# A gate of eight between the attention gathers of a graph network: two semaphores a buffer

## The chip, the cores and the metric

One core of one Trainium2 chip runs the whole program in one launch. The core has five engines with queues of their own: PE (matrix products), DVE (vector work), ACT (activations and copies), POOL (here it computes the descriptors of the indirect transfers) and SP (it only issues transfers). They share 16 DMA engines and signal one another through semaphores. The metric is device time in microseconds, as the median of several executions.

## What is computed

Eight layers over 3,125 nodes of 256 features and 103,125 edges. The change concerns only the first, an attention over the edges with 8 heads of 32 numbers:

```python
q = (nfeat @ Wq.T).reshape(n, HEADS, HEAD_DIM) / SCALING
k = (nfeat @ Wk.T).reshape(n, HEADS, HEAD_DIM)
v = (nfeat @ Wv.T).reshape(n, HEADS, HEAD_DIM)
attn = jnp.einsum('ehd,ehd->eh', k[src], q[dst])
attn = attn + attn_bias
m = jax.ops.segment_max(attn, dst, num_segments=n)
a = jnp.exp(attn - m[dst])
s = jax.ops.segment_sum(a, dst, num_segments=n)
a = a / s[dst]
out = jax.ops.segment_sum(v[src] * a[:, :, None], dst, num_segments=n)
return out.reshape(n, FEAT) @ Wo.T
```

`k[src]` and `v[src]` are read edge by edge, 2 KB for each edge (256 keys and 256 values in fp32), and they are most of what this layer moves. After it come a mixture of experts, a second graph layer and so on, up to the output.

## The kernel before, in words

A first phase sorts the nodes by their number of incoming edges and writes a table `kv` to HBM, one row of 512 numbers (key, value) for each node. `attention_phase` then works through it. Its nodes stand in 25 tiles of 128, one node on each partition. The edges of a tile are cut into **bodies** of R = 8 edges a node; a plan that is computed on the chip says how many bodies each tile has, and in the executions here there are 116.

A body `b` uses one of SETS = 4 gather buffers, `got[k]` with k = b % 4, and one of two sets v = b % 2 of everything else. A loop runs over groups of four bodies (29 here), the same on all engines:

- POOL waits for the body's indices (`index_ready`) and for its buffer (`released[k]`), and then issues eight indirect gathers (L1942), each of which brings one edge's row for each of 128 nodes: 128 x 2 KB = 256 KB. All eight raise the semaphore `gathered[k]`, by 16 each. Its waits go through `wait_apart` (L1930), which follows each wait with an increment of a semaphore of its own, so that the wait is not merged into the transfer's instruction.
- DVE waits for `gathered[k]` (L2045), multiplies keys and queries (L2046), sums over a head (L2049), takes the running maximum (L2052, L2054), and multiplies the values by the weights that ACT has exponentiated (L2057). This last operation raises `released[k]`: the buffer is free. Then it waits for ACT's `keep_ready` and for PE's `summed` of the body before, scales that sum (L2063) and raises `messages_ready` (L2065).
- PE adds the body's eight messages and the scaled earlier sum in PSUM with nine products against the identity (L1998), and raises `summed` with the last of them. The records show 18 instructions for the nine.
- ACT exponentiates (L1973 to L1978), prepares the next body's queries and biases (L1957, L1959), computes the indices for the body four later (L1952, `index_ready`), and copies the finished sum out of PSUM (L1962).
- SP stores that sum to HBM (L1914).

Ahead of the change four buffers are thus the only bound on POOL: it may run up to four bodies ahead of DVE, whatever has landed of them.

Of the kernel before, what the change touches and what calls it, by code (L numbers as in the profile page):

```python
# [63 lines left out]
def rows_at(ap):  # L64
    return bass.IndirectOffsetOnAxis(ap=ap, axis=0)
# [1346 lines left out]
R = 8  # L1412
SETS = 4
SLOTS = 64
MAIN = SLOTS // R


ALL_TILES = TILES + 3
# [18 lines left out]

ALL_BODIES = TILES * MAIN + 2 * SETS + SETS

# [36 lines left out]
def front_phase(nc, name, a, ends_dram, keys_dram, order_dram, perm, counts, natural, place, main_bodies, edges, kv_dram,  # L1476
                q_dram):

    with ExitStack() as ctx:
# [81 lines left out]
        with nc.Block() as block:  # L1561
# [147 lines left out]
            def _(dve):  # L1709
# [117 lines left out]
                table = counts[:].rearrange("p (k c) -> p k c", c=2)  # L1827
                dve.tensor_scalar(main_bodies[:], bodies[:, 0:TILES], float(MAIN), None, ALU.min)
                dve.tensor_scalar(table[:, :, N_EXTRA], bodies[0:1, :], float(MAIN), 0.0, ALU.subtract, ALU.max)
                dve.drain()  # L1830
# [14 lines left out]
def attention_phase(nc, name, a, perm, main_bodies, edges, kv_dram, q_dram, state_dram):  # L1845
# [3 lines left out]
    with ExitStack() as ctx:  # L1849
        s = Scope(nc, ctx, name)  # L1850
# [3 lines left out]
        index = [s.sb(f"index{k}", [P, R], i32) for k in range(SETS)]  # L1854
# [25 lines left out]
        plan_ready = s.sem("plan_ready")  # L1880
        q_loaded = s.sem("q_loaded")
        index_ready = s.sem("index_ready")
        gathered = [s.sem(f"gathered{k}") for k in range(SETS)]
        released = [s.sem(f"released{k}") for k in range(SETS)]
        pool_waited = s.sem("pool_waited")
        staged = s.sem("staged")
# [11 lines left out]
        def group_count(eng):  # L1898
            return eng.value_load(groups[0:1, 0:1], min_val=1, max_val=TILES * MAIN // SETS)

        with nc.Block() as block:

            @block.sync
            def _(sp):
                sp.dma_start(ident[:], a["ident"]).then_inc(const_loaded, 16)
                sp.wait_ge(plan_ready, 1)
                with sp.Fori(0, group_count(sp)) as g:
                    for k in range(SETS):
                        b = g * SETS + k
                        t = sp.value_load(tile_of[0:1, bass.ds(b, 1)], min_val=0, max_val=TILES)  # L1910
                        sp.wait_ge(out_ready, b + 3)

                        sp.wait_ge(stored, 16 * b + 32)
                        sp.dma_start(state_dram[bass.ds(t * P, P), :], out[k % 2][:]).then_inc(stored, 16)  # L1914
                sp.wait_ge(stored, group_count(sp) * (16 * SETS) + 32)
                sp.sem_inc(all_stored, 1)

            @block.gpsimd
            def _(pool):
                pool.iota(number[:], [[1, ALL_BODIES]], base=0, channel_multiplier=0, allow_small_or_imprecise_dtypes=True)  # L1920
                pool.drain().then_inc(number_set, 1)
                for k in range(SETS):
                    pool.sem_inc(released[k], 1)
                pool.sem_inc(out_ready, 1)
                pool.sem_inc(stored, 32)
                for k in range(TILES):
                    pool.indirect_dma_start(out=q[:, k, :], out_offset=None, in_=q_dram,
                                            in_offset=rows_at(perm[:, k, NODE:NODE + 1])).then_inc(q_loaded, 16)

                def wait_apart(sem, value):  # L1930


                    pool.wait_ge(sem, value)
                    pool.sem_inc(pool_waited, 1)

                wait_apart(plan_ready, 1)
                with pool.Fori(0, group_count(pool)) as g:
                    for k in range(SETS):
                        wait_apart(index_ready, g * SETS + (k + 1))
                        wait_apart(released[k], g + 1)  # L1940
                        for r in range(R):
                            pool.indirect_dma_start(out=got[k][:, r, :], out_offset=None, in_=kv_dram,  # L1942
                                                    in_offset=rows_at(index[k][:, r:r + 1])).then_inc(gathered[k], 16)

            @block.scalar
            def _(act):
                def piece(b):
                    return act.value_load(piece_of[0:1, bass.ds(b, 1)], min_val=0, max_val=TILES * MAIN - 1)

# [4 lines left out]
                def stage(b, v):  # L1954

                    at = piece(b)
                    act.activation(p_q[v][:, 0:F].rearrange("p (a n) -> p a n", a=1), q[:, bass.ds(at // MAIN, 1), :],  # L1957
                                   ACT.Copy, scale=SCALE)
# [45 lines left out]
            def _(dve):  # L2004
                def over(ap, shape, pattern, **kw):
                    return ap.rearrange(pattern, **kw).to_broadcast(shape)
# [31 lines left out]
                with dve.Fori(0, group_count(dve)) as g:  # L2038
                    for k in range(SETS):
                        b, v = g * SETS + k, k % 2  # L2040
                        keys = got[k][:, :, 0:F].rearrange("p r (h d) -> p r h d", h=HEADS)
                        values = got[k][:, :, F:2 * F].rearrange("p r (h d) -> p r h d", h=HEADS)
                        wide = [P, R, HEADS, HD]
                        dve.wait_ge(gathered[k], g * (16 * R) + 16 * R)
                        dve.wait_ge(staged, b + 1)  # L2045
                        dve.tensor_tensor(prod[v][:, :, :, 0:HD], keys,  # L2046
                                          over(p_q[v][:, 0:F], wide, "p (a h d) -> p a h d", a=1, h=HEADS), ALU.mult)
                        dve.drain()
                        dve.tensor_reduce(score[v][:, 0:R, :].rearrange("p r h -> p (r h)"),  # L2049
                                          prod[v][:].rearrange("p r h d -> p (r h) d"), AX.X, ALU.add)  # L2050
                        dve.drain()
                        dve.tensor_reduce(peak[v][:], score[v][:].rearrange("p r h -> p h r"), AX.X, ALU.max)  # L2052
                        dve.drain()
                        dve.tensor_tensor(score[v][:], score[v][:], over(peak[v][:], [P, R + 1, HEADS], "p (a h) -> p a h", a=1),  # L2054
                                          ALU.subtract).then_inc(shifted, 1)
                        dve.wait_ge(weights_ready, b + 1)
                        dve.tensor_tensor(msg[v][:, 0:R, :, 0:HD], values,  # L2057
                                          over(p_weight[v][:, 0:R * HEADS], wide, "p (r h a) -> p r h a", h=HEADS, a=1),
                                          ALU.mult).then_inc(released[k], 1)

                        dve.wait_ge(keep_ready, b + 1)
                        dve.wait_ge(summed, b + 1)
                        dve.tensor_tensor(msg[v][:, R, :, :], p_msg[1 - v][:, 0:MSG].rearrange("p (h d) -> p h d", h=HEADS),  # L2063
                                          over(keep[v][:], [P, HEADS, HD + 1], "p (h a) -> p h a", a=1), ALU.mult)
                        dve.drain().then_inc(messages_ready, 1)  # L2065
# [894 lines left out]
```

## Time and profile before

| | |
|---|---|
| Median of 3 runs | 4707.68 us |
| Lowest and highest of them | 4687.77 and 4724.29 us |
| The profiled execution | 4710.12 us, its span 4708.6 us |
| PE busy in the span | 3059.3 us (65%) |
| DVE busy | 2428.8 us (52%) |
| POOL busy | 1425.6 us (30%) |
| ACT busy | 1172.6 us (25%) |
| Moved by the DMA engines | 616.26 MB, mean 131 GB/s |

The times of instructions come from one profiled execution. A timeline counts microseconds from the start of the span. A row gives the start, the duration, the engine, the source line, the operation with its output and inputs (buffer numbers left out, so that `gnn_got` is any of the four buffers), and in brackets how long the engine had been idle before it and what the profile takes to have ended that. "issue" there means that the profile shows nothing that was waited for. A releaser is inferred from the semaphore's number, and numbers are used again by later phases: a name out of the first phase inside the attention loop is such a number's earlier use. Waits, register steps and branches are done by an engine's sequencer and have no rows of their own here.

### The profile page before, as it was taken

What the parts mean: (1) busy time and instruction counts of PE and PEld (TensorE: products, weight loads), DVE (VectorE), ACT (ScalarE), POOL (GpSimd) and SP (SyncE); (2) the same over time, 40 slices, a digit from 0 to 9 for tenths busy, and PEclk for the clock granted to TensorE, in tenths of its full rate; (3) what the DMA queues carried; (4) which work ended last, traced back from release to release, by engine and by line L of the source; (5) the groups of instructions that cost most, each with busy time, mean ns of one, the idle gap of its engine ahead of it and who ended that gap; (6) DMA issues with size and microseconds to landing.
All of it is one profiled execution on the core that took longest, in us unless ns stands there. A gap on an engine that the chain in (4) does not pass through costs nothing. (4 is left out here: it accounts for less than half of the span.)

```text
span 4708.6 us, 51834 instructions
## 1 busy us (share of the span) xinstructions
PE 3059.3 (65%) x15437; PEld 2517.8 (53%) x15437; DVE 2428.8 (52%) x4181; ACT 1172.6 (25%) x2483; POOL 1425.6 (30%) x1393
## 2 busy tenths in 40 slices
PE   4234444444444445485688873999975996499598
PEld 2123333333333334364688863777764886388587
DVE  7345555555555564443799974111133665323343
ACT  1111111111111111121255541333322553000122
POOL 4655555555555542544430000000000000001133
PEclk8667777777777777697899995999987998699799
DMA  2555555556655655243353344000017443455333
GB/s 87 160 166 171 171 171 170 168 161 174 174 168 168 174 146 197 86 71 84 109 201 167 167 168 144 17 11 11 6 51 138 140 135 108 166 205 181 124 64 53
DMA packets 293112, 616.26 MB, mean 131 GB/s; under 512 B 52284, under 2 KB 198976, under 8 KB 283040
## 3 DMA queue, kind: packets, MB, share of 16 engines
q0 software_dynamic: 105584, 294.01, 23.0%
q1 hardware_dynamic: 170080, 270.39, 16.8%
q10 hardware_dynamic: 17360, 50.80, 3.6%
q8 instruction: 42, 0.69, 0.1%
q14 instruction: 46, 0.38, 0.0%
HBM read 440.73 MB, written 176.95 MB: 131 GB/s over the span
## 5 line engine op out<-in xcount | busy, mean ns | idle before, releaser
L1998 PE MATMUL gnn_p_msg<-gnn_msg,gnn_ident 128*128 128x264 f32 x2088 | 675.0, 493 | 947.1 <-issue 710.1
L1998 PEld LDWEIGHTS gnn_p_msg<-gnn_msg,gnn_ident 128*128 128x128 f32 x2088 | 510.5, 250 | 1111.5 <-issue 737.9
L1942 POOL DMA_INDIRECT gnn_got<-kv,gnn_index x928 | 877.7, 946 | 648.0 <-DVE gnn_msg L2057 376.4
L2438 PE MATMUL tables_p_pair<-tables_spread,tables_hot 128*128 128x100 f32 x3328 | 398.0, 279 | 18.4 <-DVE tables_spread L2412 16.8
L2438 PEld LDWEIGHTS tables_p_pair<-tables_spread,tables_hot 128*128 128x128 f32 x3328 | 383.5, 194 | 32.5 <-DVE tables_spread L2412 29.9
L2063 DVE TENSOR_TENSOR gnn_msg<-gnn_p_msg,gnn_keep 128x264 f32<-128x264 f32 x116 | 49.6, 428 | 534.0 <-DMA front_w<-in_L_gnn_Wq 397.9
L2719 PE MATMUL gnn_p_sum<-gnn_hs,gnn_edge 128*128 x2500 | 288.9, 278 | 34.5 <-DVE gnn_edge L2749 34.0
L2719 PEld LDWEIGHTS gnn_p_sum<-gnn_hs,gnn_edge 128*128 128x128 f32 x2500 | 285.3, 194 | 39.3 <-issue 38.9
L2046 DVE TENSOR_TENSOR gnn_prod<-gnn_got,gnn_p_q 128x2048 f32<-128x2048 f32 x116 | 265.4, 2288 | 66.6 <-issue 34.8
L1087 PE MATMUL ffn_pA<-ffn_hw,ffn_slabs 128*128 128x256 f32 x1250 | 275.2, 382 | 32.6 <-DMA ffn_beta<-in_L_ffn_beta 32.6
L683 DVE SCALAR_TENSOR_TENSOR ffn_acc<-ffn_pC,ffn_gates,ffn_acc 128x256 f32<-128x256 f32 x200 | 88.9, 480 | 395.8 <-PE ffn_pC L567 395.8
L487 ACT ACTIVATE ffn_h<-ffn_pA,ffn_hb,ffn_hs 128x384 f32<-128x384 f32 (+1 forms) x320 | 197.4, 617 | 352.9 <-PE ffn_pA L537 352.9
L2057 DVE TENSOR_TENSOR gnn_msg<-gnn_got,gnn_p_weight 128x2048 f32<-128x2048 f32 x116 | 265.5, 2289 | 34.1 <-issue 19.4
L2049 DVE TENSOR_REDUCE gnn_score<-gnn_prod 128x64 f32<-128x2112 f32 x116 | 272.9, 2353 | 8.6
L1087 PEld LDWEIGHTS ffn_pA<-ffn_hw,ffn_slabs 128*128 128x128 f32 x1250 | 238.3, 191 | 65.3 <-DMA ffn_beta<-in_L_ffn_beta 33.0
L2749 DVE SCALAR_TENSOR_TENSOR gnn_edge<-gnn_steep,gnn_cell 128x1152 f32<-128x1152 f32 (+1 forms) x150 | 190.5, 1270 | 132.6 <-PE gnn_p_sum L2719 80.3
L2410 DVE TENSOR_TENSOR tables_hot<-tables_low_c,tables_iota 128x1024 f32<-128x1024 f32 x208 | 253.5, 1219 | 0.0
L2695 ACT ACTIVATE gnn_steep<-gnn_number,gnn_minus 128x1152 f32<-128x1152 f32 (+1 forms) x150 | 177.4, 1184 | 151.8 <-DVEq L2751 115.5
L976 POOL DMA_INDIRECT by_expert<-ffn_xn,ffn_place_i x100 | 97.7, 977 | 374.3 <-DVEq L1258 346.1
L1962 ACT ACTIVATE gnn_out<-gnn_p_msg 128x264 f32<-128x264 f32 x117 | 45.7, 390 | 599.1 <-issue 530.0
L567 PE MATMUL ffn_pC<-ffn_wc,ffn_h 128*128 128x256 f32 x800 | 190.7, 396 | 4.4 <-DVE ffn_acc L672 4.4
L148 POOL MEMSET h_epsb<- 128x1 f32 x1 | 0.1, 98 | 624.3 <-POOLq L51 624.3
(413 smaller groups left out, 4802.8 us busy)
## 6 DMA issues: line engine op xcount, KB each, us to landing
weight_table<-tables_weight_slab SPq DMA_DIRECT2D x13, 3200.0 KB
count_table<-tables_count_row SPq DMA_DIRECT2D x13, 3200.0 KB
ffn_slabs<-weight_table SPq DMA_DIRECT2D x25, 1600.0 KB
gnn_cell<-count_table ACTq DMA_DIRECT2D x50, 576.0 KB, 3.8
state<-gnn_out SPq DMA_DIRECT2D x116, 136.0 KB
ffn_xs<-by_expert SPq DMA_DIRECT2D x60, 260.0 KB, 3.3
gnn_got<-kv,gnn_index POOLq DMA_INDIRECT x928
ffn_x<-x SPq DMA_DIRECT2D x20, 640.0 KB
```

The source lines that it names most:

```text
L487: act.activation(to[:, m, t0 * P:t1 * P], pA[:, j % 4, 0:(t1 - t0) * P], hidden_act[layer][0], bias=hb[layer][:, e, m:m + 1], scale=scale) ...
L567: last = nc.tensor.matmul(pC[:, t * F:(t + 1) * F], last_h[:, k, t * P:(t + 1) * P], wc[:, e, k, :], start=(k == 0), stop=(k == KC - 1))
L1087: last = nc.tensor.matmul(pA[j % 2][:, 0:F], slabs[:, j % SLABS, b * P:(b + 1) * P], hw[:, b, :], start=(b == 0), stop=(b == TILES - 1))
L1942: pool.indirect_dma_start(out=got[k][:, r, :], out_offset=None, in_=kv_dram, in_offset=rows_at(index[k][:, r:r + 1])).then_inc(gathered[k] ...
L1998: last = nc.tensor.matmul(p_msg[v][:, 0:MSG], ident[:], msg[v][:, r].rearrange("p h d -> p (h d)"), start=(r == 0), stop=(r == R))
L2046: dve.tensor_tensor(prod[v][:, :, :, 0:HD], keys, over(p_q[v][:, 0:F], wide, "p (a h d) -> p a h d", a=1, h=HEADS), ALU.mult)
L2049: dve.tensor_reduce(score[v][:, 0:R, :].rearrange("p r h -> p (r h)"), prod[v][:].rearrange("p r h d -> p (r h) d"), AX.X, ALU.add)
L2057: dve.tensor_tensor(msg[v][:, 0:R, :, 0:HD], values, over(p_weight[v][:, 0:R * HEADS], wide, "p (r h a) -> p r h a", h=HEADS, a=1), ALU.mu ...
L2410: dve.tensor_tensor(hot[c % AHEAD][:], across_tiles(low_c[:, at], CHUNK, P), counting(CHUNK, P), ALU.is_equal)
L2438: last = nc.tensor.matmul(at, hot[c % AHEAD][:, r, :], spread[c % AHEAD][:, r, :], start=True, stop=True)
L2719: last = nc.tensor.matmul(p_sum[:, to:to + C], of[:, b * P:(b + 1) * P], rhs.rearrange("p a d -> p (a d)"), start=False, stop=False)
L2749: dve.scalar_tensor_tensor(edge[v][:, 0:w], steep[v][:, 0:w], 1.0, cell[k][:, 0:w], ALU.min, ALU.mult).then_inc(edge_ready, 1)
```

## The change

The gathers of a buffer raise two semaphores in place of one, the first four (half 0) and the last four (half 1). Ahead of each half of the buffers k = 1, 2 and 3 POOL now also waits until the same half of the buffer k - 1, of the same group, has landed. Buffer 0 has no such wait. DVE waits for both halves ahead of its first product, where it waited for one count.

```diff
+HALF_R = R // 2
...
-        gathered = [s.sem(f"gathered{k}") for k in range(SETS)]
+        gathered = [[s.sem(f"gathered{k}{h}") for h in range(2)] for k in range(SETS)]
...
                         wait_apart(index_ready, g * SETS + (k + 1))
                         wait_apart(released[k], g + 1)
                         for r in range(R):
+                            if k > 0 and r % HALF_R == 0:
+                                wait_apart(gathered[k - 1][r // HALF_R], g * (16 * HALF_R) + 16 * HALF_R)
                             pool.indirect_dma_start(out=got[k][:, r, :], out_offset=None, in_=kv_dram,
-                                                    in_offset=rows_at(index[k][:, r:r + 1])).then_inc(gathered[k], 16)
+                                                    in_offset=rows_at(index[k][:, r:r + 1])).then_inc(gathered[k][r // HALF_R], 16)
...
-                        dve.wait_ge(gathered[k], g * (16 * R) + 16 * R)
+                        for h in range(2):
+                            dve.wait_ge(gathered[k][h], g * (16 * HALF_R) + 16 * HALF_R)
                         dve.wait_ge(staged, b + 1)
```

On POOL, the buffers 0, 1 and 2 in the loop's body stand as follows. The semaphores in brackets go by the names under which the first phase used their numbers: `front_keys_loaded0` is `index_ready`, and the other one is `released[k]`. Before:

```order
L1942 DMA gnn0_got<-kv,gnn0_index0 128x512 [waits front_start_ready]
L1942 DMA gnn0_got<-kv,gnn0_index0 128x512 x7
L1933 REGISTER_ALU
L1942 DMA gnn0_got<-kv,gnn0_index1 128x512 [waits front_keys_loaded0,front_next_ready]
L1942 DMA gnn0_got<-kv,gnn0_index1 128x512 x7
L1933 REGISTER_ALU
L1942 DMA gnn0_got<-kv,gnn0_index2 128x512 [waits front_keys_loaded0,front_mine_ready]
L1942 DMA gnn0_got<-kv,gnn0_index2 128x512 x7
```

And with the change, where `front_keys_loaded1` and `front_keys_loaded2` are the two halves of buffer 0, `front_keys_loaded3` and `front_keys_loaded4` those of buffer 1:

```order
L1945 DMA gnn0_got<-kv,gnn0_index0 128x512 [waits front_place_ready]
L1945 DMA gnn0_got<-kv,gnn0_index0 128x512 x7
L1934 REGISTER_ALU
L1934 ISA [waits front_keys_loaded0,front_scattered]
L1945 DMA gnn0_got<-kv,gnn0_index1 128x512 [waits front_keys_loaded1]
L1945 DMA gnn0_got<-kv,gnn0_index1 128x512 x3
L1945 DMA gnn0_got<-kv,gnn0_index1 128x512 [waits front_keys_loaded2]
L1945 DMA gnn0_got<-kv,gnn0_index1 128x512 x3
L1934 REGISTER_ALU
L1945 DMA gnn0_got<-kv,gnn0_index2 128x512 [waits front_keys_loaded0,front_perm_loaded,front_keys_loaded3]
L1945 DMA gnn0_got<-kv,gnn0_index2 128x512 x3
L1945 DMA gnn0_got<-kv,gnn0_index2 128x512 [waits front_keys_loaded4]
```

The eight gathers of buffers 1 and 2 are now two runs of four with a wait ahead of each; those of buffer 0 are as they were.

On DVE, the start of a body (k = 1) stands so before, `front_keys_loaded2` being `gathered[1]` and `front_scattered` being `staged`:

```order
L2045 REGISTER_ALU [waits front_keys_loaded2]
L2046 TENSOR_TENSOR gnn0_prod1<-gnn0_got,gnn0_p_q1 128x64x32 [waits front_scattered]
```

And with the change, where `front_done` is `staged`:

```order
L2049 REGISTER_ALU [waits front_keys_loaded4,front_keys_loaded3]
L2050 TENSOR_TENSOR gnn0_prod1<-gnn0_got,gnn0_p_q1 128x64x32 [waits front_done]
```

The register step has two waits in place of one; the operations behind it are unchanged, and nothing moves between engines.

## Rows read from the trace of the kernel before

**Rows 1.** Table of stretches: busy us (count) by engine, clock, DMA share, GB/s
```profile
core 0: us, PE busy (x) PEld busy (x) DVE busy (x) ACT busy (x) POOL busy (x), PEclk, DMA share, GB/s
240.00:1765.00 1525.00, 665.15 (x2053) 503.08 (x2054) 895.17 (x690) 268.33 (x1063) 865.02 (x915) 0.72 0.58 168
```

**Rows 2.** Groups by line, 235 to 1773 us: count, busy us, mean ns, idle before
```profile
L1942 POOL DMA_INDIRECT gnn_got<-kv,gnn_index x919 | 869.2, 946 | 645.3 <-DVE gnn_msg L2057 376.4 <-issue 267.6 <-ACT gnn_index L1952 1.2
L2049 DVE TENSOR_REDUCE gnn_score<-gnn_prod 128x64 f32<-128x2112 f32 x116 | 272.9, 2353 | 8.6
L2057 DVE TENSOR_TENSOR gnn_msg<-gnn_got,gnn_p_weight 128x2048 f32<-128x2048 f32 x116 | 265.5, 2289 | 34.1 <-issue 19.4 <-ACT gnn_p_weight L1973 14.7
L2046 DVE TENSOR_TENSOR gnn_prod<-gnn_got,gnn_p_q 128x2048 f32<-128x2048 f32 x116 | 265.4, 2288 | 66.6 <-issue 34.8 <-DMA gnn_got<-kv,gnn_index 31.8
L2063 DVE TENSOR_TENSOR gnn_msg<-gnn_p_msg,gnn_keep 128x264 f32<-128x264 f32 x116 | 49.6, 428 | 534.0 <-DMA front_w<-in_L_gnn_Wq 397.9 <-issue 136.1
```

**Rows 3.** Waits, 235 to 1773 us: total us, times, longest us
```profile
DVE gnn_msg L2063 <- DMA front_w<-in_L_gnn_Wq: 397.9, 28, 27.8
POOL gnn_got L1942 <- DVE gnn_msg L2057: 376.4, 44, 20.9
DVE gnn_msg L2063 <- issue: 136.1, 10, 15.1
DVE gnn_prod L2046 <- DMA gnn_got<-kv,gnn_index: 31.8, 2, 30.0
```

**Rows 4.** Timeline of one cycle: start us, us, engine, line, operation, idle before
```profile
1025.40 0.43 DVE L2063 TENSOR_TENSOR gnn_msg<-gnn_p_msg,gnn_keep 128x264 f32<-128x264 f32 x1 [16.42 <-DMA front_w<-in_L_gnn_Wq]
1033.92 0.42 DVE L2063 TENSOR_TENSOR gnn_msg<-gnn_p_msg,gnn_keep 128x264 f32<-128x264 f32 x1
...
1034.79 0.94 POOL L1942 DMA_INDIRECT gnn_got<-kv,gnn_index  x1 [12.61 <-DVE gnn_msg L2057]
...
1042.44 0.42 DVE L2063 TENSOR_TENSOR gnn_msg<-gnn_p_msg,gnn_keep 128x264 f32<-128x264 f32 x1
1042.95 6.64 PE L1998 MATMUL gnn_p_msg<-gnn_msg,gnn_ident 128*128 128x264 f32 x18 [4.24 <-issue]
1043.08 2.29 DVE L2046 TENSOR_TENSOR gnn_prod<-gnn_got,gnn_p_q 128x2048 f32<-128x2048 f32 x1 [0.21 <-issue]
1048.75 2.29 DVE L2057 TENSOR_TENSOR gnn_msg<-gnn_got,gnn_p_weight 128x2048 f32<-128x2048 f32 x1 [0.29 <-issue]
1048.94 0.30 ACT L1978 ACTIVATE gnn_msg<-gnn_score 128x64 f32<-128x64 f32 x1
1062.33 0.43 DVE L2063 TENSOR_TENSOR gnn_msg<-gnn_p_msg,gnn_keep 128x264 f32<-128x264 f32 x1 [11.29 <-DMA front_w<-in_L_gnn_Wq]
1063.34 2.29 DVE L2046 TENSOR_TENSOR gnn_prod<-gnn_got,gnn_p_q 128x2048 f32<-128x2048 f32 x1 [0.58 <-issue]
1063.60 0.95 POOL L1942 DMA_INDIRECT gnn_got<-kv,gnn_index  x1 [0.30 <-issue]
1072.10 0.94 POOL L1942 DMA_INDIRECT gnn_got<-kv,gnn_index  x1 [7.55 <-DVE gnn_msg L2057]
```

**Rows 5.** Timeline of the burst before that one: two buffers' boundaries and the end
```profile
1002.38 0.95 POOL L1942 DMA_INDIRECT gnn_got<-kv,gnn_index  x1 [0.30 <-issue]
1011.34 0.21 ACT L1952 ACTIVATE gnn_index<-edges 128x8 int32 x1 [3.25 <-issue]
1012.49 0.94 POOL L1942 DMA_INDIRECT gnn_got<-kv,gnn_index  x1 [0.42 <-issue]
1021.24 0.94 POOL L1942 DMA_INDIRECT gnn_got<-kv,gnn_index  x1 [0.30 <-issue]
```

**Rows 6.** Timeline of the loop's start: the eighth gather, and DVE's first product
```profile
232.15 0.95 POOL L1942 DMA_INDIRECT gnn_got<-kv,gnn_index  x1 [0.30 <-issue]
235.94 2.29 DVE L2046 TENSOR_TENSOR gnn_prod<-gnn_got,gnn_p_q 128x2048 f32<-128x2048 f32 x1 [30.04 <-DMA gnn_got<-kv,gnn_index]
```

**Rows 7.** The line L2046: ns min/median/max, first and last start us
```profile
L2046 DVE TENSOR_TENSOR gnn_prod<-gnn_got,gnn_p_q x116: 2286/2289/2290, 235.9 to 1764.8; 128x2048 f32<-128x2048 f32 x116
```

**Rows 8.** Table of stretches, columns as in rows 1: inside a burst and at its end
```profile
1001.00:1006.00 5.00, 5.00 (x18) 3.80 (x17) 4.85 (x3) 1.17 (x1) 3.78 (x4) 0.76 0.81 234
1006.00:1011.00 5.00, 0.19 (x1) 0.00 (x0) 2.61 (x3) 1.41 (x7) 3.78 (x4) 0.92 0.72 211
1016.00:1021.00 5.00, 0.00 (x0) 0.00 (x0) 0.00 (x0) 0.00 (x0) 3.78 (x4) 0.50 0.77 212
1023.00:1024.00 1.00, 0.00 (x0) 0.00 (x0) 0.00 (x0) 0.00 (x0) 0.00 (x0) 0.50 0.78 234
1024.00:1025.00 1.00, 0.00 (x0) 0.00 (x0) 0.00 (x0) 0.00 (x0) 0.00 (x0) 0.50 0.13 49
1025.00:1026.00 1.00, 0.09 (x1) 0.09 (x1) 0.43 (x1) 0.11 (x1) 0.00 (x0) 0.50 0.00 0
```

## Prediction

> **What bounds the kernel now.** I read the table of stretches first. The attention loop, from 240 to 1765 us, is 1,525 of the 4,708.6 us, and in it no engine is full: DVE is busy for 895 us, POOL for 865 us, PE for 665 us, and the DMA engines for 0.58 of the time [rows 1]. Outside it nothing is edited. Then the groups by line, for what one body costs (a body is 8 gathers of 128 rows into one of four buffers, and the arithmetic on them). The 919 gathers counted there take 946 ns each; DVE's three large operations take 2.3 us each; and DVE stands idle for 534.0 us ahead of L2063, in a loop of 116 bodies [rows 2]. The waits say who was waited for: POOL stood for 376.4 us until DVE's L2057 released a buffer, and DVE stood for only 31.8 us, twice, for a gather; its idle time at L2063 is 28 + 10 = 38 stalls of 14 us [rows 3]. So gathered data is almost never late, and POOL's idle time is DVE's stall handed back through the four buffers.
>
> One cycle shows how. DVE runs three bodies 8.52 us apart (L2063 at 1025.40, 1033.92, 1042.44), ends L2057 at 1051.04 and then stands until 1062.33 [rows 4]. L2063 waits in the code for ACT's `keep_ready`, last raised by the operation that ended at 1049.24, and for PE's `summed`, raised by a product whose 18 records end at 1049.59. Both had ended by then. The label "DMA front_w" on that row is an old user of a semaphore number and no transfer that L2063 waits for. That PE's is the late one, by 12.7 us, is my reading: ACT's signals pass in a stall (its index of 1011.55 starts a gather at 1012.49, while DVE stands [rows 5]). POOL meanwhile issues 24 gathers without a break, every 1.25 us from 1034.79 to 1063.60, then has no free buffer until DVE ends another L2057, and starts again at 1072.10. The cycle is thus 9.4 us from DVE's restart at 1025.40 to POOL's at 1034.79, and then the burst of 24 x 1.25 = 30 us, less what DVE restarts before its end (2.5 us here): 37 us in this one, and over the loop 1,529 us (L2046 from 235.94 to 1764.8 [rows 6, 7]) in 38 stalls, 40 us. Why PE's signal is late no row says. It is late only in the second half of a burst, and it comes near the burst's end.
>
> **The change part by part.** The gate is the first part. Six half-buffers of a group (k = 1, 2, 3, two halves each) get a wait, 6 x 29 groups = 174. The gate of a half asks for the same half of the buffer before. The last gather of that half started five gathers earlier, 5 x 1.25 = 6.25 us. When has a gather landed? Two places bound it. In the first body the eighth gather starts at 232.15 and DVE, which waits for just that, starts at 235.94 [rows 6]: 3.8 us. At the end of a burst the last gather starts at 1021.24, the DMA engines are at 0.78 until 1024, 0.13 until 1025 and 0.00 after it [rows 5, 8]: at most 3.8 us again. So the neighbour's half is down 6.25 - 3.8 = 2.45 us before the gated gather would start anyway. How early must it be? The gather at 1012.49 is one that waited, for the index that ACT's operation at 1011.34 gives after 0.21 us: 0.94 us from signal to start, with an idle of 0.42 us in place of 0.30. The boundary of two buffers eight gathers before it, at 1002.38, had the same two waits already met and stands at 0.30 like every other gather [rows 5]. So a met wait costs POOL nothing, because it lies under the gather that runs, and the gate has 2.45 - 0.94 = 1.5 us to spare. After a break of POOL the neighbour is older still. With 3.8 us from start to landing and one start each 1.25 us, about three gathers are in flight at any time; a bound of eight does not bind. I take 0 for the gates. The bounds: 174 x 0.12 us = 21 us if each costs what the late index cost, and no gain, if nothing in the burst moves.
>
> The Trainium skill's page "DMA: Bandwidth & Descriptors", section "Anatomy of one DMA — SWDGE (gpsimd) path", speaks against any gate of this kind: a transfer's fixed cost is mostly the receipt of its last write, which the semaphore has to wait for, about 2.0 us beside the bytes at 436 GB/s. A gate puts that receipt on the issuing engine's path. For these 256 KB an estimate from the page is 2.6 us, less than the 3.8 us that the rows show, and by either the gate opens in time.
>
> DVE's wait is the second part: one wait ahead of L2046 becomes two (one each half), 116 times, each met long before in the loop. There the idle time is 0.21 us in most bodies and 0.58 us after a jump back, and it holds a drain's end, a register step and the wait [rows 4]. The trace has no row for one wait alone. From below it costs nothing; from above the whole 0.21 us again, 116 x 0.21 = 24 us. I take a third, 0.07 us, because the gap is made of three things: 8 us. Only one body in three has DVE ahead of POOL's restart, so a third of that, 3 us, is what the cycle sees if the stall absorbs the rest. Between 3 and 8 us I take 6. PE, ACT and SP keep their orders; four more semaphores are cleared in the same place.
>
> The sum against the profiled execution: 1.5 us around the span, 4708.6 + 1.5 + 0 + 6 = 4716. That execution is 2.4 us over the median of the three runs (4707.68), so against the median it is 4714. The runs lie from 4687.77 to 4724.29, and a difference under 1% is what cannot be told from none here.
>
> **The rivals.**
> The gate calms the burst (faster). The stall belongs to bursts: PE's signal was quick at 1034 and 1042 and late after twelve gathers in a row, while the DMA engines stood at 0.72 to 0.81 [rows 8]. If the gates broke the stream often enough, the signal would not be late. Without any stall POOL sets the pace, 116 x 8 x 1.25 = 1,160 us in place of 1,529: 369 us less, 4347. With half of the stalls gone it is 4530. Against it: a gate that opens 1.5 us early breaks nothing. 13 in 100, most of it for a part of the gain.
> The gate binds (slower). It decides from the point where a gather needs more than 6.25 - 0.94 = 5.3 us from its start to a landing that POOL can see. In the burst nobody waits for a gather, so the 3.8 us come from its two ends alone. If it were 6.3 us in its middle, every gate would cost 1 us: 174 us, 4890; at 5.8 us it is 87 us, 4803. For it speaks only that one signal, PE's, is late just there; against it that the bytes keep moving at over 200 GB/s to the end and nothing is left a microsecond after 1024 [rows 8]. 11 in 100.
> The rhythm locks otherwise. The stalls come once in three bodies (38 in 116 bodies). If a small shift of the waits made it one in four, 9 fewer would be 126 us less (4590); one in two, 20 more would be 280 us more (4996). Nothing in the rows asks for either. 3 in 100 each way.
> The added waits cost their upper bounds: 21 + 24 = 45 us, 4755. This is inside the forecast's own range and just within 1%.
>
> **How the numbers follow.** The forecast, 4714, that the gates are met and nothing moves, has 70 in 100; its own range is 4680 to 4758, from the spread of the runs and the upper bounds of the waits. The calmed burst has 13, the binding gate 11, the other rhythm 6. Faster by over 1% is the first rival and half of the last but one: 0.16. Slower is the second and the other half: 0.14. Within 1%: 0.70. For 8 in 10 the range reaches down to a third of the stalls gone, 4714 - 369 / 3 = 4591, said as 4600, and up to gates at a little under half a microsecond each, 4714 + 76 = 4790.
>
> **What the profile of the changed kernel would show.** If I am right: gathers 1.25 us apart across half-buffer boundaries, with an idle of 0.30 us; bursts of 24; DVE's idle ahead of L2063 (now L2067) still near 534 us in some 38 stalls; POOL waiting for L2057 (now L2061) for some 376 us; no idle time of POOL put down to a DMA. Ahead of the first product of a body DVE would show near 0.28 us in place of 0.21. I am wrong at the gates if POOL shows waits on its own gathers, and wrong about the burst if the stalls grow fewer or shorter while its gathers keep their spacing. Wrong altogether would be a loop of 116 bodies that ends before 1650 us or after 1850 us.

## The result and the profile after

The changed kernel takes 4720.66 us in the median (20 runs, 4691.24 to 4738.19), the kernel before 4706.90 us in 20 runs of the same sessions: a ratio of 1.0031, 95% interval 1.0019 to 1.0042. So it is about 14 us slower, 9 to 20 us, and within 1%. The forecast was 4714.

The profiled execution has a span of 4715.9 us. Its page shows the same busy times as before, and its attention loop, from the first to the last start of DVE's first product, is 1,541.0 us where it was 1,528.9 [rows 7]. That is 12 us more; the rest of the span is 5 us less. The line, as the profile tells it by source line (ns min/median/max, first and last start us):

```profile
L2050 DVE TENSOR_TENSOR gnn_prod<-gnn_got,gnn_p_q x116: 2286/2289/2291, 234.7 to 1775.7; 128x2048 f32<-128x2048 f32 x116
```

The groups by line, 235 to 1785 us, with columns as in rows 2; the edit moved every line by three or four:

```profile
L1945 POOL DMA_INDIRECT gnn_got<-kv,gnn_index x918 | 868.0, 946 | 652.6 <-DVE gnn_msg L2061 370.3 <-issue 275.3 <-ACT gnn_index L1955 4.0
L2053 DVE TENSOR_REDUCE gnn_score<-gnn_prod 128x64 f32<-128x2112 f32 x116 | 272.9, 2353 | 8.5
L2061 DVE TENSOR_TENSOR gnn_msg<-gnn_got,gnn_p_weight 128x2048 f32<-128x2048 f32 x116 | 265.5, 2289 | 34.1 <-issue 19.1 <-ACT gnn_p_weight L1976 15.0
L2050 DVE TENSOR_TENSOR gnn_prod<-gnn_got,gnn_p_q 128x2048 f32<-128x2048 f32 x116 | 265.5, 2289 | 74.4 <-issue 42.6 <-DMA gnn_got<-kv,gnn_index 31.9
L2067 DVE TENSOR_TENSOR gnn_msg<-gnn_p_msg,gnn_keep 128x264 f32<-128x264 f32 x116 | 49.6, 428 | 537.8 <-DMA front_rows_in<-in_x 386.8 <-issue 151.0
```

Against [rows 2] two numbers on DVE have moved: the idle time ahead of the first product by 7.8 us (66.6 to 74.4), and that ahead of the operation with the stalls by 3.8 us (534.0 to 537.8). POOL waits for DVE's release for 370.3 us, where it was 376.4. The waits of the same stretch (total us, times, longest):

```profile
DVE gnn_msg L2067 <- DMA front_rows_in<-in_x: 386.8, 28, 27.0
POOL gnn_got L1945 <- DVE gnn_msg L2061: 370.3, 38, 21.0
DVE gnn_msg L2067 <- issue: 151.0, 12, 14.6
POOL gnn_got L1945 <- DMA gnn_got<-kv,gnn_index: 3.0, 10, 0.3
```

The last row looks like gates that bind, but its longest is 0.3 us, the ordinary idle time between two gathers: a landing happened to fall into it. A piece of one cycle (timeline):

```profile
1017.79 0.94 POOL L1945 DMA_INDIRECT gnn_got<-kv,gnn_index  x1 [0.30 <-issue]
1018.39 2.29 DVE L2061 TENSOR_TENSOR gnn_msg<-gnn_got,gnn_p_weight 128x2048 f32<-128x2048 f32 x1 [0.29 <-issue]
1019.04 0.95 POOL L1945 DMA_INDIRECT gnn_got<-kv,gnn_index  x1 [0.30 <-issue]
...
1032.79 0.95 POOL L1945 DMA_INDIRECT gnn_got<-kv,gnn_index  x1 [0.30 <-issue]
1035.04 0.43 DVE L2067 TENSOR_TENSOR gnn_msg<-gnn_p_msg,gnn_keep 128x264 f32<-128x264 f32 x1 [14.36 <-DMA front_rows_in<-in_x]
1035.75 2.29 DVE L2050 TENSOR_TENSOR gnn_prod<-gnn_got,gnn_p_q 128x2048 f32<-128x2048 f32 x1 [0.28 <-issue]
1044.59 0.94 POOL L1945 DMA_INDIRECT gnn_got<-kv,gnn_index  x1 [10.86 <-DVE gnn_msg L2061]
```

It is the picture of [rows 4]: gathers every 1.25 us across all half-buffer boundaries (the median idle time ahead of a gather is 0.305 us at each of the eight places in a buffer, before and after), DVE stalled from the end of L2061 (1020.68) to 1035.04, POOL without a buffer until 1044.59. The gap ahead of DVE's product is 0.28 us, where it was 0.21.

### The profile page after: what moved, and what is told of

Read it like the earlier page. It is cut to its first block and busy times, and to the rows that moved or that the text cites. A ratio compares the mean times of both kernels' runs of the same rounds, so it can differ in the third digit from the quotient of the medians.

```text
span 4715.9 us, 52153 instructions
## 1 busy us (share of the span) xinstructions
PE 3051.7 (65%) x15437; PEld 2515.0 (53%) x15437; DVE 2429.5 (52%) x4181; ACT 1172.7 (25%) x2483; POOL 1425.3 (30%) x1393
## 2 busy tenths in 40 slices
DMA packets 293112, 616.26 MB, mean 131 GB/s; under 512 B 52284, under 2 KB 198976, under 8 KB 283040
## 5 line engine op out<-in xcount | busy, mean ns | idle before, releaser
L1945 POOL DMA_INDIRECT gnn_got<-kv,gnn_index x928 | 877.4, 946 | 655.6 <-DVE gnn_msg L2061 370.3
L2067 DVE TENSOR_TENSOR gnn_msg<-gnn_p_msg,gnn_keep 128x264 f32<-128x264 f32 x116 | 49.6, 428 | 537.8 <-DMA front_rows_in<-in_x 386.8
L2050 DVE TENSOR_TENSOR gnn_prod<-gnn_got,gnn_p_q 128x2048 f32<-128x2048 f32 x116 | 265.5, 2289 | 74.4 <-issue 42.6
L2061 DVE TENSOR_TENSOR gnn_msg<-gnn_got,gnn_p_weight 128x2048 f32<-128x2048 f32 x116 | 265.5, 2289 | 34.1 <-issue 19.1
```

The lines of the kernel that those rows point to most:

```text
L2050: dve.tensor_tensor(prod[v][:, :, :, 0:HD], keys, over(p_q[v][:, 0:F], wide, "p (a h d) -> p a h d", a=1, h=HEADS), ALU.mult)
L2061: dve.tensor_tensor(msg[v][:, 0:R, :, 0:HD], values, over(p_weight[v][:, 0:R * HEADS], wide, "p (r h a) -> p r h a", h=HEADS, a=1), ALU.mu ...
```

## The experiments

Three sessions, each with runs of the kernel before on its own chip; ratios are against those. Only the session of the result has a trace of the kernel before, so an idle time that is set beside [rows 2] is compared across sessions; in the first of the three the kernel before takes 4730.07 us in the median, 23 us more than above. A diff is cut to the line that makes the experiment; what goes with it elsewhere (more semaphores and DVE's waits on them, another operand, the zeroing) is left out. Two questions: what the 14 us are made of, and whether a gate could do more than this one.

### The two parts, each alone

DVE's second wait without the gates, an edit of the changed kernel:

```diff
-                            if k > 0 and r % HALF_R == 0:
-                                wait_apart(gathered[k - 1][r // HALF_R], g * (16 * HALF_R) + 16 * HALF_R)
```

> The change without its gates: two semaphores a buffer, and DVE waits for both, POOL waits for none of its own gathers. Theory (the cost of the change is DVE's second wait, the gates are met and free): DVE's idle time ahead of its first product stays at the 74 us of the changed kernel, against 67 us before, and the time is that of the changed kernel, 10 to 16 us over before. Rival (the gates cost it): the time is that of before, within 5 us.

Measured: 4737.66 against 4730.07 us, a ratio of 1.0015, interval 0.9997 to 1.0032: 8 us more, between -1 and 15. The idle time ahead of DVE's product is 74.3 us, as in the changed kernel, so the second wait is 0.07 us in each body. That part of the theory holds. The time decides nothing: 8 us lies between the theory's 10 to 16 and the rival's 5, and the interval takes in both, and none at all.

POOL's waits without DVE's, to the kernel before:

```diff
+                            if k > 0 and r % (R // 2) == 0:
+                                wait_apart(released[k], g + 1)
```

> The kernel before with six more waits a group on POOL at the places of the gates, each for a semaphore that the same engine has already waited for (the buffer's release), so that each is met. Theory: a met wait lies under the gather that runs; gathers stay 1.25 us apart and the time is that of before, within 5 us. Rival (the gates cost POOL time by being there): up to 174 x 0.12 = 21 us more, with idle times of 0.42 us at half-buffer boundaries.

Measured: 4741.64 us, a ratio of 1.0023, interval 1.0009 to 1.0037: 11.6 us more, 4 to 17. Neither side of the expectation holds as it was put: the median idle time ahead of a gather is still 0.305 us at each half-buffer boundary, as the theory has it, and yet the kernel is slower, by more than the theory's 5 us in the median (5 us is inside the interval). To see whether this is real, the same wait stands ahead of seven of each body's eight gathers (`if r > 0:`), 812 in all:

> The kernel before with seven more waits a body on POOL, each long met: 812 in place of the change's 174. Theory (a met wait lies under the gather that runs, and what the six a group cost was noise): within 8 us of before. Rival (each instruction or signal on POOL inside a burst adds to what holds the others back, 11.6 us for 174): 4.7 times as much, 40 to 60 us over before.

Measured: 4747.29 against 4710.72 us, a ratio of 1.0084, interval 1.0061 to 1.0107: 37 us more by the medians, 40 by the ratio, 29 to 50 by the interval. The theory falls, and the rival holds at the low end of its 40 to 60 us. The groups by line of this kernel, 235 to 1810 us:

```profile
L1944 POOL DMA_INDIRECT gnn_got<-kv,gnn_index x919 | 869.2, 946 | 674.0 <-DVE gnn_msg L2059 378.6 <-issue 285.3 <-ACT gnn_index L1954 10.1
L2065 DVE TENSOR_TENSOR gnn_msg<-gnn_p_msg,gnn_keep 128x264 f32<-128x264 f32 x116 | 49.6, 428 | 562.8 <-DMA front_w<-in_L_gnn_Wq 456.6 <-issue 105.8 <-PE gnn_p_msg L2000 0.2
```

Inside a buffer POOL's gathers are no further apart (0.305 us of idle time in the median at each place). Ahead of a buffer's first gather they are, now and then: 21 of the 116 idle times there lie between 0.35 and 4 us, where 4 do in the trace before and 4 in the changed kernel, and POOL's "issue" time is 285.3 us where it was 267.6. By the timelines each of the 21 ends a microsecond or less after that buffer's index or its release, as for the late index of the prediction. One of them (timeline, ACT's index at L1954):

```profile
1028.27 0.21 ACT L1954 ACTIVATE gnn_index<-edges 128x8 int32 x1 [3.42 <-issue]
1029.42 0.94 POOL L1944 DMA_INDIRECT gnn_got<-kv,gnn_index  x1 [0.61 <-issue]
```

On DVE only the idle time at the stall grew, 562.8 us against 534.0 in [rows 2], and that is the whole of the 29 us by which the loop is longer (1,557.9 us against 1,528.9). So a met wait on POOL costs about 0.05 us (39 / 812), and it is paid on other engines: in DVE's stall, and in indices of ACT that come late. Two things stay open. Each of these waits stands with an increment of a semaphore (`wait_apart`), and no run parts the two. And the stall differs between sessions too: 559.0 us in the half-bytes kernel below, which has no wait added. For 174 gates 0.05 us each is 8 us; the run of the 174 alone says 11.6, and its interval, 4 to 17 us, holds both.

### What the stall is made of

Three kernels change one suspected load each. First the bytes: rows of 1 KB out of the query table in place of 2 KB.

```diff
-                            pool.indirect_dma_start(out=got[k][:, r, :], out_offset=None, in_=kv_dram,
+                            pool.indirect_dma_start(out=got[k][:, r, 0:F], out_offset=None, in_=q_dram,
```

> The kernel before, whose gathers bring 1 KB rows of the query table in place of 2 KB rows of keys and values, with as many gathers of as many rows; DVE reads the same half twice. Theory (what holds PE's signal back is the load of the bytes on the DMA engines): the stalls of 14 us ahead of L2063 are gone or much shorter, POOL is the bound at 10 us a body, and the loop takes 1,160 to 1,250 us in place of 1,529: 4,340 to 4,430. Rival (it is the number of packets, signals or records in a burst, not their bytes): the stalls stay, 4,700.

Measured: 4721.01 us, 0.9975 (0.9958 to 0.9993). The rival holds: half of the gathered bytes are worth 0.25%. The waits of this kernel, 235 to 1800 us:

```profile
DVE gnn_msg L2063 <- DMA front_w<-in_L_gnn_Wq: 507.6, 34, 28.5
POOL gnn_got L1942 <- DVE gnn_msg L2057: 397.5, 37, 20.8
DVE gnn_msg L2063 <- issue: 51.3, 4, 12.9
```

38 stalls, as before, and 559 us. Then PE's own instructions, two products in place of nine:

```diff
-                        for r in range(R + 1):
+                        for r in (0, R):
```

> The kernel before with two products a body on PE in place of nine (messages 1 to 7 are left out of the sum, and the weights in the denominator's column are ones). Theory A (the late signal waits behind something of PE's own instructions, 0.7 us for each of its 18, which gives 13 us): the stall shrinks with them to about 3 us, and the loop goes toward POOL's 1,160 us, 4,350 to 4,450 in all. Theory B (the signal is held until the burst of gathers ends, whatever PE did): each stall still ends near the burst's end, and the time stays within 1% of before.

Measured: 4512.66 us, 0.9537 (0.9512 to 0.9562). Theory B falls: the stalls ahead of L2063 are gone (1.1 us of idle time in all). Theory A has that right, but not the total of 4,350 to 4,450: the loop is 1,346 us and not 1,160, because the hold has gone to another engine. A timeline inside a burst:

```profile
1011.78 2.13 PE L1998 MATMUL gnn_p_msg<-gnn_msg,gnn_ident 128*128 128x264 f32 x4 [10.00 <-issue]
1017.91 0.39 ACT L1957 ACTIVATE gnn_p_q<-gnn_q 128x256 f32 x1 [6.77 <-issue]
1019.31 0.32 ACT L1959 ACTIVATE gnn_prod<-edges 128x64 f32 x1 [1.01 <-issue]
1019.66 2.29 DVE L2046 TENSOR_TENSOR gnn_prod<-gnn_got,gnn_p_q 128x2048 f32<-128x2048 f32 x1 [7.96 <-issue]
1024.71 0.94 POOL L1942 DMA_INDIRECT gnn_got<-kv,gnn_index  x1 [6.79 <-ACT gnn_index L1952]
```

Between its operations ACT has only a register to load in the code, and yet it is 6.77 us late; DVE waits for ACT, and POOL then waits for ACT's index (174.6 us in this kernel, 1.2 us before). That index is a second bound on POOL, beside the four buffers. So the stall is not a property of PE's products alone. My reading is that in a burst the instructions of several engines go through slowly, and that PE, which has the most of them in a body, shows it first; the rows show late ones on ACT and SP, and PE's late signal.

Last the number of gathers, four a body in place of eight:

```diff
-                        for r in range(R):
+                        for r in range(0, R, 2):
```

> The kernel before with four gathers a body in place of eight (every other edge's row is not fetched; the buffers are zeroed once, about 70 us ahead of the loop, and the arithmetic is unchanged). Half the bytes did not help while the packets stayed; here packets, bytes and POOL's time all halve. Theory (the number of transfers' packets in a stretch holds the other engines back): no stalls, DVE's 8.5 us a body is the bound, 116 x 8.5 = 990 us for the loop, 4,240 in all. Rival (something in the loop apart from the gathers causes the stall): stalls of 14 us once in three bodies stay, 4,750.

Measured: 4179.59 us, 0.8856 (0.8830 to 0.8881). The theory holds, though the total was put 60 us too high: the zeroing hides ahead of the loop, whose first product starts at 234.2 us (235.9 before). The loop is 996 us, DVE is the bound at 8.6 us a body, and the row that had 534.0 us of idle time has none (groups by line, 225 to 1250 us):

```profile
L2066 DVE TENSOR_TENSOR gnn_msg<-gnn_p_msg,gnn_keep 128x264 f32<-128x264 f32 x116 | 49.4, 426 | 0.0
```

So it is the number of gathers in a stretch that goes with the stalls, and not their bytes alone. Nor is it the DMA packets that the page counts: of 293,112 the half-bytes kernel has lost 30,816 and this one 37,120, nearly as many, and only this one has lost its stalls.

SP issues one store a body, and its issues tell of the stalls too, by their longest and not by their median. The row in the kernel before, in the one with 812 more waits, and with half of the gathers (ns min/median/max):

```profile
L1914 SPq DMA_DIRECT2D state<-gnn_out x116: 6/697/2087, 269.5 to 1778.1; - x116
```

```profile
L1914 SPq DMA_DIRECT2D state<-gnn_out x116: 8/336/1424, 270.5 to 1807.2; - x116
```

```profile
L1914 SPq DMA_DIRECT2D state<-gnn_out x116: 332/332/370, 258.2 to 1243.8; - x116
```

In the six kernels with stalls of 534 us and more the median is 692 to 700 ns three times and 336 to 339 three times, but the longest is 1,400 ns or more in each; in the four without them or nearly so (half of the gathers, spaced gathers, and two kernels with gates that bind, below) it is 370 to 719 ns.

### Gates that bind

The same gate at other distances. At one gather's distance, four in flight at most, each half waits for the one just before it:

```diff
-                            if k > 0 and r % HALF_R == 0:
-                                wait_apart(gathered[k - 1][r // HALF_R], g * (16 * HALF_R) + 16 * HALF_R)
+                            if r % HALF_R == 0 and (k, r) != (0, 0):
+                                j = 2 * k + r // HALF_R - 1
+                                wait_apart(gathered[j // 2][j % 2], g * (16 * HALF_R) + 16 * HALF_R)
```

> The gate at one gather's distance: each half waits for the half issued just before it, seven gates a group of four bodies, so that at most four gathers are in flight. My rule for a gate at a distance of d gathers is a cost of 3.8 + 0.94 - 1.25 d us if positive: 3.5 us here. Theory (nothing else moves): 203 gates x 3.5 us = 710 us more work for POOL, 1,870 us for the loop, about 340 us over before: 5,050 to 5,100. Rival (broken bursts free the other engines, the stalls of 14 us vanish and POOL's gates are all that is left): the same bound of POOL, 1,160 + 710 = 1,870, so the total tells little, but the stalls ahead of DVE's L2066 operation show it: none in place of 38. If the stalls stayed on top of the gates the loop would be over 2,200.

Measured: 5005.59 us, 1.0606 (1.0575 to 1.0637), a little under the forecast of my rule. Its timeline of POOL gives the gate's true price:

```profile
1001.70 0.95 POOL L1946 DMA_INDIRECT gnn_got<-kv,gnn_index  x1 [0.30 <-issue]
1002.95 0.95 POOL L1946 DMA_INDIRECT gnn_got<-kv,gnn_index  x1 [0.30 <-issue]
1007.37 0.94 POOL L1946 DMA_INDIRECT gnn_got<-kv,gnn_index  x1 [3.47 <-DMA gnn_got<-kv,gnn_index]
```

4.42 us from a gather's start to the start of one that waits for it, 3.17 us a gate (not 3.5), since 1.25 of the 4.42 pass in any case. Less the 0.94 us from signal to start, a gather is seen as landed 3.5 us after its start. The loop is 1,817 us; 1,160 + 203 x 3.17 is 1,804. There is no stall: DVE's idle time ahead of that operation is 0.0 us, and it waits for its gathers instead (896.4 us). Broken bursts do free the other engines, but here POOL pays more than they gain.

At three gathers' distance, with four semaphores a buffer and a gate ahead of each pair:

```diff
+                            if r % 2 == 0 and 4 * k + r // 2 >= 2:
+                                j = 4 * k + r // 2 - 2
+                                wait_apart(gathered[j // 4][j % 4], g * 32 + 32)
```

> Four semaphores a buffer, and each pair of gathers waits for the pair before the last one, 14 gates a group: the last gather of that pair started three gathers earlier, at most four gathers in flight. By my rule 3.8 + 0.94 - 3.75 = 1.0 us a gate, 406 gates, 400 us of POOL's time. Theory (POOL's idle time of about 370 us takes it in, the stalls shrink as the stream thins): 4,650 to 4,750. Rival (the landing that POOL sees is quicker than 3.8 us and the gate is free): as the changed kernel plus two more waits on DVE, 4,735 to 4,760.

Measured: 4601.79 us in two runs, 0.975 (0.9689 to 0.9811), under the 4,650 to 4,750 of the theory. It was run again for a closer interval:

> The kernel of the gate at three gathers' distance (14 gates a group, four semaphores a buffer) once more, with an interval. Theory (its gates of about 0.5 us each thin the stream so far that PE's signal is held back for less long): faster than before by 2 to 3%. Rival (its two first runs were lucky, the first of them 0.5% from the second): within 1% of before.

Measured: 4617.41 against 4710.72 us, 0.9787 (0.9756 to 0.9819): the theory holds. A gate that binds costs about 0.5 us, not 1.0 (one gather starts 4.32 us after the one that it waits for, 1004.13 to 1008.45, where three spacings are 3.75 us); POOL waits for DVE's release for 126.5 us in place of 376.4, and the stalls' idle time fell to 408 us, in more stalls that are shorter (49 of 8 us, where there were 38 of 14). With the gates ahead of every fourth gather only (`r % 4 == 0`):

> The same with a gate ahead of every fourth gather only, at three gathers' distance: 7 gates a group of about 0.5 us, POOL at 11 us a body, between the 10 of before and the 12 of 14 gates. Theory (the stalls follow the density of the gathers): between the two, 1 to 2% faster than before. Rival (the gain of the 14 gates is in the first thinning, and each gate past it only costs POOL): 3% or more faster than before.

Measured: 4638.08 us, 0.9851 (0.9826 to 0.9876), with 426 us of idle time at the stalls: between the two, as the theory has it. Then evenly, a semaphore for each gather, and each waits for the third before it:

```diff
+                            if 8 * k + r >= 3:
+                                j = 8 * k + r - 3
+                                wait_apart(gathered[j // 8][j % 8], g * 16 + 16)
```

> A semaphore for each of a buffer's eight gathers, and each gather waits for the third before it, at most three in flight. The gate opens 4.3 us after the start of the gather that it waits for (the starts of the kernels with gates at one and three gathers' distance), so starts are 4.3 / 3 = 1.4 us apart, 11.5 us a body, evenly. Theory (the density decides, and even is better than in pairs): as good as 14 gates or better, 2 to 4% faster than before, less 0.5 us a body (60 us) for seven more waits on DVE where DVE is the bound. Rival (each instruction more in a burst holds the others back further): slower than the 14 gates by over 1%.

Measured: 4546.00 us (4538.37 to 4551.23), 0.9645 (0.9624 to 0.9666): 165 us under the kernel before, and the fastest kernel here that computes everything. The theory holds, with eight waits a body on DVE in it. Its groups by line, 235 to 1620 us:

```profile
L1946 POOL DMA_INDIRECT gnn_got<-kv,gnn_index x920 | 868.8, 944 | 498.2 <-issue 382.6 <-DMA gnn_got<-kv,gnn_index 91.6 <-ACT gnn_index L1956 24.1
L2051 DVE TENSOR_TENSOR gnn_prod<-gnn_got,gnn_p_q 128x2048 f32<-128x2048 f32 x116 | 265.4, 2288 | 416.8 <-DMA gnn_got<-kv,gnn_index 407.2 <-issue 9.6
L2068 DVE TENSOR_TENSOR gnn_msg<-gnn_p_msg,gnn_keep 128x264 f32<-128x264 f32 x116 | 49.4, 425 | 26.6 <-remote 13.7 <-issue 12.9
```

The stalls are gone (26.6 us in place of 534.0), POOL no longer waits for DVE, and DVE waits for gathers: the bound is now POOL's pace. The loop is 1,368 us, 11.8 us a body; 4.3 / 3 = 1.43 us a gather makes 11.5.

One experiment missed its aim:

> The kernel before with a fill of 256 numbers a partition on POOL ahead of each gather, so that gathers come further apart (1.5 to 1.8 us in place of 1.25). Theory (the stalls come of the density of the gather stream): they vanish or shrink, and the loop is bound by POOL at 12 to 14 us a body; at 1.5 us a gather it is 1,400 us, 130 us under before. Rival (the stalls come of a burst's length, not its density): the stalls stay at 14 us on longer bursts, and the loop is 15% or more longer, 4,950.

Measured: 6988.73 us, where 4,950 was the highest forecast. The fill is followed by a drain, so each gather came 4.1 us after the one before in place of 1.5 to 1.8 (timeline of POOL: starts at 1002.43 and 1006.56). That is past anything the question was about. No stall was left (0.0 us of idle time at L2066, the operation that was L2063), which agrees with the rest and decides nothing.

## Why the prediction was right, and where it was off

- **The gate of eight is met everywhere.** Right, by the idle time of 0.30 us at its places. The sign "no idle time of POOL put down to a DMA" came out otherwise to the letter, in 10 places of 0.3 us that are the ordinary ones. The landing was put at 3.8 us and is 3.5 by the kernel at one gather's distance, so the gate opens 6.25 - 4.4 = 1.8 us early. The estimate from the Trainium skill's page ("DMA: Bandwidth & Descriptors", "Anatomy of one DMA — SWDGE (gpsimd) path") was 2.6 us, which is too short by 0.9 us here. The 3.5 us count from the start of POOL's own 0.95 us of work on the gather.
- **"So a met wait costs POOL nothing ... I take 0 for the gates."** This is the step that was off. At the change's 174 places POOL's idle time is the usual 0.305 us in the median, as I said, but a met wait costs the loop about 0.05 us, paid on the engines that are held back; for the 174 that is 8 us (11.6 by their own run), inside the bound of 21 that I gave and then did not use. I looked for the price only on the engine that waits, and only at the place of the wait.
- **DVE's second wait, 0.07 us.** Right to the hundredth (0.28 against 0.21 us; 7.8 us in all). I let the stall absorb part of it and took 6; the run of it alone says 8, but with an interval from -1 to 15, so the price in time rests on the rows.
- **The sum.** 6 us were forecast and 14 measured. The parts give 8 + 8 = 16 us with the gates at 0.05 us, and 19 with the gates' own run; the trace of the changed kernel shows 7.8 us at the product and 3.8 at the stall. The intervals are too wide to part these. The forecast's own range allowed either sign, and 4714 came within 7 us of 4720.66 partly because both terms are so small: the mechanism (met gates, nothing moves) is what the rows confirm, not the 6 us.
- **"The gate calms the burst"**: the right mechanism at the wrong distance. This gate breaks nothing, so it gains nothing. A gate that binds does what the rival said, and its gain is capped by its own price on POOL: 369 us without stalls and without a price, 161 us of the loop for the best one tried.
- **"The gate binds"** falls. Two gathers behind a gate have more idle time than usual and less than a stall's, 1.33 and 3.04 us, and both start about a microsecond after their buffer's index or release (1184.17 after the index of 1183.13, 1316.61 after the release of 1315.72).
- **"The rhythm locks otherwise"** did not happen (40 stalls, 38 before). "Bursts of 24" is nearly so: 30 of the 44 unbroken runs of gathers are of 24, where 36 of 38 were. In four buffers the second gather starts after 1.67 us of idle time; the kernel of DVE's second wait alone has five such places, and neither the kernel before nor the one of the 174 met waits has any, so it seems to go with the two semaphores and not with the gates.
- **"Why PE's signal is late no row says."** The runs say this much: it follows the number of gathers in a stretch, not the bytes, and not PE alone; with fewer instructions of PE it is ACT that is late. Through what these things hang together no run here shows. How far the recording of an execution takes part is open too; the profiled executions are as long as the others (4710.12 us against a median of 4707.68).

## What to carry to other kernels

Before a bound on transfers in flight is added, work out from the trace how many are in flight: here 3.5 us to a landing and 1.25 us between starts make three in flight, and a bound of eight only adds its waits. If the aim is to thin a stream, choose the distance from start-to-start time (4.4 us over the number in flight) and spread the gates evenly. And look for the price of an instruction in a stalled loop on the engines that stall, not only on the one that gets it.

## What was not expected of the hardware

- Half of the gathered bytes in as many gathers of as many rows changed the time by 0.25%; half of the gathers took 11% off the whole program, 35% off the loop.
- In a burst of gathers 1.25 us apart other engines' small steps take longer, now and then: SP's issue of a store up to 2,087 ns, where the longest is 370 ns with half of the gathers. Its median is no measure of this: 697 ns in the kernel before and 336 in one with longer stalls.
- Waits that are long met (each here with an increment of a semaphore behind it) are not free in such a loop: 812 of them on POOL cost 29 to 50 us, and within a buffer POOL's gathers are as far apart as before.
